# Two stacked attention and mixture layers: loads and a store on two queues, slot one-hots compared instead of transposed, gate mask by match-replace

## What is computed

```python
# 1: cross-attention, one head, over 256 context rows of 96 features per batch
# 2: first mixture: 64 experts of width 88, top 6 of softmax scores + bias, capacity 64
scores = softmax(xf @ gate_w.T);  _, idx = top_k(scores + gate_b, 6)
weights = take_along_axis(scores, idx)
pos = place of the token among those of its expert, in token order   # dropped from 64 on
h = silu(xb @ w1.T) * (xb @ w3.T);  y = scatter_add(weights * (h @ w2.T))
z = (silu(xf @ ws1.T) * (xf @ ws3.T)) @ ws2.T        # shared expert of width 176
out = y + z
# 3: cross-attention, 16 heads of 8 features, same context
# 4: second mixture: 8 experts of width 512, top 2, capacity 160 by rank
```

## Time and profile before

| | us |
|---|---|
| median of 3 runs | 389.87 (389.84 to 390.15) |
| span of the profiled execution | 390.5 |
| PE busy in it | 319.4 (82%) |
| DVE busy | 250.5 (64%) |
| ACT busy | 193.9 (50%) |
| POOL busy | 132.0 (34%) |
| mean granted PE clock | 0.882 of full speed |

### The profile page before, as it was taken

How to read it: one execution, slowest core, us unless ns; L and a number is a source line. 1 busy time by engine, 2 the same in 40 slices (tenths; PEclk the granted TensorE clock), 3 DMA queues, 4 the chain that set the end, 5 groups by cost and what they waited for, 6 DMA issues and landing times.

```text
span 390.5 us, 6230 instructions
## 1 busy us (share of the span) xinstructions
PE 319.4 (82%) x2260; PEld 216.6 (55%) x2260; DVE 250.5 (64%) x571; ACT 193.9 (50%) x355; POOL 132.0 (34%) x150
## 2 busy tenths in 40 slices
PE   0678777817879879799736999999989899999995
PEld 0447434305757667677611345554567677777763
DVE  0456799502563463444658877866388889988876
ACT  1135332102243044044322477778679788888882
POOL 4248259074223303570630442011010534443200
PEclk9989668555898899899975599999999999999998
DMA  3861564336654453560042330003000021000001
GB/s 104 217 189 62 95 87 55 55 35 35 128 121 44 126 124 40 119 170 2 0 94 57 76 79 2 4 3 111 1 0 2 20 89 55 2 1 0 3 0 55
DMA packets 12348, 24.00 MB, mean 61 GB/s; under 512 B 1988, under 2 KB 7004, under 8 KB 11997
## 3 DMA queue, kind: packets, MB, share of 16 engines
q1 hardware_dynamic: 11293, 21.50, 22.0%
q0 software_dynamic: 1024, 2.10, 6.9%
HBM read 20.88 MB, written 2.62 MB: 60 GB/s over the span
## 4 chain that ended last, share of the span: by engine, by line
PE 58%; DMA 15%; DVE 14%; ACT 6%; issue 3%; POOL 3%; SPq 0%; DVEq 0%; POOLq 0%; ACTq 0%
PE bank L757 50%; DMA normalised<-xn 8%; DMA x<-in_x 3%; PE bank L956 3%; DMA xg<-normalised,slot_token 2%; DVE score L1600 2%; DVE pbuf L1403 2%; DVE xn L1275 2%; DMA big<-q_parts 1%; PE bank L906 1%; ACT splits L646 1%; PE bank L968 1%; POOL rstd L452 1%; DVE st L1262 1%; POOL big L514 1%
## 5 line engine op out<-in xcount | busy, mean ns | idle before, releaser
L757 PE MATMUL bank<-frbuf,splits 128*128 128x512 f32 x384 | 95.7, 399 | 1.3 <-DVE frbuf L1646 0.9
L757 PEld LDWEIGHTS bank<-frbuf,splits 128*128 128x128 f32 x384 | 69.8, 188 | 21.2 <-issue 5.3
L1646 DVE TENSOR_TENSOR frbuf<-pbuf,frbuf 128x512 fp32r<-128x512 f32 x64 | 52.3, 826 | 11.9 <-ACT pbuf L751 11.4
L504 POOL DMA_INDIRECT xg<-normalised,slot_token x32 | 30.6, 955 | 65.2 <-DVE slot_token L1423 47.8
L1600 DVE TENSOR_REDUCE score<-bank 128x2 f32<-128x512 f32 x64 | 42.0, 687 | 14.5 <-PE bank L757 13.8
L747 ACT ACTIVATE frbuf<-bank,biases 128x512 fp32r<-128x512 f32 x64 | 44.2, 691 | 13.1 <-PE bank L757 9.7
L723 ACT ACTIVATE pbuf<-bank 128x512 f32<-128x512 f32 x64 | 37.1, 598 | 15.6 <-PE bank L757 15.3
L1429 DVE CAST splits<-bank 128x1024 fp32r<-128x1024 bf16 x16 | 19.6, 1225 | 39.1 <-PE bank L757 27.7
L751 ACT ACTIVATE pbuf<-bank,biases 128x512 f32<-128x512 f32 x64 | 43.7, 683 | 0.0
L757 PE MATMUL bank<-splits,frbuf 128*128 128x512 f32 (+1 forms) x144 | 38.2, 424 | 0.8 <-ACT frbuf L668 0.8
L640 ACT COPY ctxT<-bank 128x512 f32<-128x512 f32 x8 | 4.7, 586 | 67.6 <-PE bank L906 50.1
(11 more groups left out here) (197 smaller groups left out, 512.1 us busy)
## 6 DMA issues: line engine op xcount, KB each, us to landing
big<-in_w SPq DMA_DIRECT2D x8, 704.0 KB
ew<-in_ew SPq DMA_DIRECT2D x16, 256.0 KB, 3.3
big<-in_w SPq DMA_DIRECT2D x8, 352.0 KB
ks<-k_parts SPq DMA_DIRECT2D x8, 256.0 KB
big<-q_parts SPq DMA_DIRECT2D x8, 192.0 KB
k_parts<-parts SPq DMA_DIRECT2D x1, 768.0 KB, 3.9
x<-in_x SPq DMA_DIRECT2D x1, 512.0 KB, 13.1
normalised<-xn SPq DMA_DIRECT2D x2, 256.0 KB, 18.3
```

The costliest lines, as they stand in the source:

```text
L504: pool.indirect_dma_start(out=xg[:, g % 2, j, :], out_offset=None, in_=xn_dram, in_offset=bass.IndirectOffsetOnAxis(ap=slot_token[:, g % 3 ...
L757: return pe.matmul(out_, lhsT, rhs, start=start, stop=stop, skip_group_check=True)
L1646: v.tensor_tensor(out=actl[:, n % NA, :], in0=act[:, n % 4, :], in1=acth[:, n % NA, :].bitcast(F32), op=ALU.subtract).then_inc(f_lo, 1)
```

## The change

It has five parts.

1. *Queues.* `ctxT` and `packc` are issued by ACT, `packc` as 96 partitions and 1. SP begins with x, in two halves with a semaphore each, for which DVE waits one after the other. The two halves of the row store are issued by ACT. The eight key-stack loads no longer stand ahead of them: SP issues two behind the weights of each of the groups 3 to 6.
2. *Slot-by-token one-hots.* The 32 transposes per group and their copies go. POOL writes the numbers 0 to 1023 into each partition once (`iota_t`, in `ew`), and DVE compares them with the slot's token number, one `tensor_scalar` of 128x1024 per chunk, as fp32r into one of now two `PTs` buffers (`slot_onehots`). For that it waits until the combine two groups back is done.
3. *Order of the loop.* Gathered rows are transposed into bank 3 and the hidden rows into bank 4, so that bank 7 holds outputs alone; hidden transposes come ahead of gathered ones. `dispatch(g + 3)` and `slot_onehots(g + 1)` stand ahead of `yl(g)` on DVE; the token-by-slot one-hots have two buffers instead of three.
4. *Shared expert.* The four products go from POOL to DVE, and its output matmuls from ahead of the first gathered rows to the first pass of the loop. Its silu has four buffers in `ew`.
5. *Gate mask.* `biased` gets two more columns that hold a sentinel. The seventh and eighth largest are overwritten by it, `match_replace` replaces the first match of each of the eight values, and the mask is where the result differs.

Core of the diff:

```diff
-            sp.dma_start(ctxT[0:CD, :], ctx_in).then_inc(ld_ctx, 16)
-            sp.dma_start(packc[:, :, :], packc_in).then_inc(ld_packc, 16)
-            sp.dma_start(x[:, :, :], x_in.rearrange("(c p) d -> p c d", p=P)).then_inc(ld_x, 16)
+            for h2 in range(2):
+                sp.dma_start(x[:, 4 * h2:4 * h2 + 4, :],
+                             x_in.rearrange("(c p) d -> p c d", p=P)[:, 4 * h2:4 * h2 + 4, :]
+                             ).then_inc(ld_x[h2], 16)
...
             for g in range(RING0, NG):
                 sp.wait_ge(e_Y, g - RING0 + 1)
                 group_weights(g)
+                if g < RING0 + NCOMB // 2:
+                    keys_stacked(2 * (g - RING0))
+                    keys_stacked(2 * (g - RING0) + 1)
...
+            a.dma_start(ctxT[0:CD, :], ctx_in).then_inc(ld_ctx, 16)
+            a.dma_start(packc[0:CD, :, :], packc_in[0:CD]).then_inc(ld_packc, 16)
+            a.dma_start(packc[CD:CD + 1, :, :], packc_in[CD:CD + 1]).then_inc(ld_packc, 16)
+            def normalised_rows(h2):
+                a.wait_ge(ln_out, 3 + h2)
+                a.dma_start(xn_dram.rearrange("(c p) d -> p c d", p=P)[:, 4 * h2:4 * h2 + 4, :],
+                            xn[:, 4 * h2:4 * h2 + 4, :]).then_inc(xn_out, 16)
...
+            row_i = xg[:, :, :, :].rearrange("p a j d -> p (a j d)").bitcast(I32)
+            chained(pool.iota(row_i, pattern=[[1, T]], base=0, channel_multiplier=0))
+            pool.tensor_copy(iota_t, row_i).then_inc(c_iota, 1)
...
+                chained(v.memset(top8[:, cs, K0:8], sentinel))
                 for c in range(first, first + 4):
-                    ins = v.max_index(out=idx8[:, c, :], in_max=top8[:, c, :],
-                                      in_values=biased[:, c, :])
+                    ins = v.match_replace(out=rest[:, c - first, :], in_to_replace=top8[:, c, :],
+                                          in_values=biased[:, c, :], imm_value=-sentinel)
                 chained(ins)
...
+                v.tensor_tensor(out=selb[:, cs, :], in0=rest[:, 0:4, 0:E0], in1=biased[:, cs, 0:E0],
+                                op=ALU.not_equal).then_inc(g_sel, 1)
...
+            def slot_onehots(g):
+                v.wait_ge(e_id, g + 1)
+                if g >= 2:
+                    v.wait_ge(e_comb, g - 1)
+                for j in range(NPAIR):
+                    ins = v.tensor_scalar(PTs[g % 2][:, j, :], iota_t, token_f[:, g % 3, j:j + 1],
+                                          None, ALU.is_equal)
+                ins.then_inc(e_PT, 1)
```

More of the change, by code:

```diff
@@ L489, in _ @@
             pool.wait_ge(g_parts, 2)
-            for i in range(4):
-                part = hs[i // 2][:, half(i % 2)]
-                pool.wait_ge(sh_sil, i + 1)
-                pool.tensor_tensor(out=part, in0=part, in1=shared_silu(i),
-                                   op=ALU.mult).then_inc(sh_sb, 1)
-            pool.wait_ge(sh_sb, 4)
             pool.wait_ge(xn_out, 32)
@@ L1434, in _ @@
             dispatch(1, range(4, 8))
-            dispatch_even(0, 0)
+            shared_product(0)
             slot_values(1)
             dispatch(2)
+            for i in range(1, 4):
+                shared_product(i)
+            v.wait_ge(c_iota, 1)
+            slot_onehots(0)
             for g in range(NG):
```

166 lines of the change are left out of this document (65 added, 101 removed).

## The result

| | before | changed |
|---|---|---|
| median, us (runs) | 389.86 (387.70 to 390.15, 4) | 362.22 (359.64 to 363.86, 4) |
| ratio to before, 95% interval | 1 | 0.9283 (0.9222 to 0.9344) |
| span of the profiled execution | 390.5 | 357.6 |
| PE / DVE / POOL busy | 82% / 64% / 34% | 83% / 70% / 39% |
| mean granted PE clock | 0.882 | 0.899 |

The change saves 27.6 us where the forecast of 346 stood for 43.9; 362.2 lies 2.2 above the range's end. (In every timed run on record that lists both, the time is 1.7 to 2.1 us above the span; by that a span of 390.5 belongs to a run of some 392.4, an estimate, and the median is 389.9.)

A forecast was written before the change was run, and what follows sets the result against it. Matmuls hold half the chain, but in the loop neither PE nor DVE is full: steps wait on each other. 9.0 + 14.4 - 4.1 + 24.1 = 43.4; 390.5 - 43.4 - 0.6 = 346.5, forecast 346 us, range 336 to 360.

The forecast's parts named there:

- Start, 9.0: Before the first matmuls: packc lands at 6.3 us, second transposes start at 13.2 instead of 22.11; gain 9.0 us.
- Gate and way in, 14.4: From gate mask to first gather: 2.0 from mask, 3.0 from products; first gather 14.4 us earlier, bounds 12 and 16.
- The step for the store: Before the first gather: row store goes out from ACT's queue with nothing in front, so rows arrive in time.
- First pass, gives back 4.1: First pass of the loop: shared outputs, 7.9 us, now stand in it; outputs end at 89.5; gives back 4.1 us.
- The slow clock: First pass: PE's clock taken at half, 0.50 as from 66 to 99 us before; at full clock nothing given back.
- The loop, 24.1: Seven passes at 8.8 us plus 1 for the clock: 62.6 instead of 86.7, gain 24.1 us; bounds 13 and 29.
- The floor of PE: Loop: PE's work at full clock, 8.1 us a pass; 8.8 was taken for losses between two full engines.
- The rival of the key stack: Loop: stack loads ahead of the weights make the last group's weights land 10 us late; 356 us, chance 0.09.
- The rival of the shared port: Loop: every DVE compare first waits for one gather's issue, passes of 10.5 us; 358 us, chance 0.18.
- POOL's delay of 3.0 falls in the slack: Loop, port rule read one way only: POOL is delayed by 3.0 us, the slack covers it, time stays 346.
- After the loop: From the last outputs to the end: nothing changes, no gain or loss.
- - 0.6: End of the sum: the profiled span of 390.5 lies 0.6 above the median run, so 0.6 us is subtracted.

The follow-up runs named there:

- e3_stack_early: Changed kernel with the eight key-stack loads back where they stood before the change, right behind the store of the key parts; 363.9 us (0.9255).
- e9_ones_by_act: Changed kernel with key-stack loads half early, half behind the last gathers, slot numbers ahead of hidden rows, and POOL's fill of ones given to ACT; 342.8 us.
- e5_stack_half: Changed kernel with four key-stack loads behind the store of the key parts, four after the last group's gathered rows are transposed; 354.8 us.
- e2_dispatch_behind: Changed kernel with dispatch(g + 3) behind the slot-by-token compares on DVE instead of ahead of them; 359.1 us.
- e14_half_ones_act: Changed kernel with key-stack loads half early, half behind the last gathers, and POOL's fill of ones given to ACT; slot numbers stay behind hidden rows; 351.7 us.
- e15_best_dispatch_behind: e9_ones_by_act with dispatch(g + 3) behind the slot-by-token compares on DVE; 362.7 us.

## Why the prediction was wrong

1. **Start, 9.0: right in the trace, partly for another reason.** packc landed at 7.40, not 6.3, within the bounds. The loads are worth 5.7 (median) to 7.0 (trace); most of the rest of the profiled difference was a clock that had fallen in the run before.
2. **Gate and way in, 14.4: right.** 23.6 with the start against 23.4. The mask was worth 2.9 (forecast 2.0, for PE was no longer between), the products 3.6 (3.0). The step for the store ("with nothing in front") held because no stack load ran beside it; `e3_stack_early` shows that ACT's queue alone would not have done it.
3. **First pass, gives back 4.1: right in size.** Outputs at 81.4 against 80.5 (89.5 less the 9.0 of the start). Rows came 3 later, the pass itself was shorter, 15.5 instead of 17.5. The slow clock that the forecast took for it was there, but it is no given: with the slot numbers first the same stretch took 10.7 (66.6 to 77.3 in `e9_ones_by_act`).
4. **The loop, 24.1: this failed; it gained 14.7.** The step was "Gathered rows come 7.8 us after the token numbers and are needed some 11 after them", with 3 us of slack. That 7.8 came from the first group before, whose gathers went out when the stack and the row store were through. In the changed kernel the same distance is 15 to 19 us in the slow passes (94.6 to 111.4; 118.2 to 136.7). The stack loads cost 7.4 us of the kernel's time (`e5_stack_half`): with none of them beside a gather the seven passes take 63.9, near the 62.6 forecast. What the slow first issue costs is not settled (`e2_dispatch_behind`: 3.2 in the median, nothing in the trace). Beside the weights alone the rows still come 12.3 to 13.9 after the first issue (e3): with the 6.8 ahead of it that is 19 to 21 for two passes, 9.6 to 10.4 each, where 8.1 was the floor. That part goes only when the gathers start earlier (`e9_ones_by_act` against `e14_half_ones_act`: 3.9 in the loop, beside 4.0 in the first pass). And three of the four long waits are paid again in clock.
   The floor of PE was right: 57.9 for seven passes in `e9_ones_by_act`, with the same work in a slightly other order, against 61.6 forecast, and compares at 0.73 to 0.75 against 0.74.
5. **The rival of the key stack named the right transfers and the wrong victim.** It priced late weights; those are needed three passes on and never came late. The gathers, needed within two, did. It had taken gathers only as something that slows the stack.
6. **The rival of the shared port** was right about the lock and wrong about who blocks: no gather's issue held up a compare by more than 0.25 us; DVE's two-input dispatch held up the issue. The Trainium skill ("SBUF — State Buffer", SBUF: two separate sides) says that whoever starts first holds the pair for the whole instruction and the other blocks. The traces agree for two pairs of operations: a dispatch compare stretched an issue from 0.94 to 2.75, POOL's fills four compares from 2.75 to 11.12. For a gather's issue beside the slot-by-token compares they show next to nothing of it (1.02 instead of 0.94). I had read the rule for gathers alone and not looked for fills beside the compares, and "POOL's delay of 3.0 falls in the slack" failed with the slack.
7. **After the loop**: unchanged, 204 us, right.

The sum closes so. The forecast's terms stand for a span of 347.1 (390.5 less 43.4), and 357.6 was measured, 10.5 more: 9.4 in the loop, 0.9 in the first pass, 0.2 behind it. From 10.5 to the 15.7 between 346.5 and 362.2 it is another 5.2. Half of that is the conversion "- 0.6": a run's time lies 2.0 above its span in the changed kernel, so the term had the wrong sign: the profiled execution before was longer than most. The other half is that the profiled run of the changed kernel lies 2.6 below its median; what the other runs lose more is not known, as they have no trace.

## What to carry to other kernels

When a transfer is moved off a critical queue, list every latency-bound transfer that it will now run beside, and price the time until those land with that company, not alone; a separate queue does not separate the engines, and the size of the other transfer's packets sets how long a turn is. Where a loop's data come through a chain over several passes, add that chain up beside the floors of the engines, and take the longer. And before a DVE operation goes from PSUM to SBUF operands, look for every fill and gather of POOL that can meet it: the faster loop moves them onto each other.

## What the runs showed of the hardware

- A store and gathers in queues of their own landed behind stack loads that another queue had issued before them: the store after 30.4 us instead of 2.3, gathers after 7.5 to 25 us, by the table above. The Trainium skill ("DMA: Bandwidth & Descriptors", Queues, rings and completion order) has each engine go round its queues packet by packet. The packet records agree: beside stack packets of 32 KB and some 4 us, one 4 KB packet of the gathers, or two 512-byte ones of the store, got its turn. Turns of such unequal length give the small transfers almost nothing. Beside the store the stack moved 68 GB/s at a DMA share of 0.57 (`e3_stack_early`):

```profile
42.00:46.00 4.00, 3.39 (x14) 1.42 (x14) 3.77 (x12) 2.59 (x4) 2.09 (x3) 0.57 0.57 68
```

- POOL's fills and DVE's f32 compares within SBUF exclude each other for the whole length of a fill (2.75 us became 11.12), while a gather's issue beside the same compares takes 1.02 instead of 0.94 and leaves the four at 2.74 to 2.95.
- A gather's issue beside a two-input bf16 compare takes until 0.8 us after that compare ends.
- A wait of 3.0 us in a full pass cost 5.4 (`e15_best_dispatch_behind`): the mean granted clock was 0.76 there instead of 1.00. Of four waits of 2.2 to 3.2 us in the changed kernel three were followed by a stretch at 0.50, one by none.
